# A vision tower with two routed expert layers: a first batch of 9 tiles, and its fixed units among the last tiles' routing

## The chip, the cores and the metric

The kernel runs on one core of a Trainium2 chip. The core has the engines TensorE (PE, matrix products; its weight loads are PEld), VectorE (DVE), ScalarE (ACT), GpSimd (POOL) and the sync engine (SP), each with its own in-order instruction stream; they meet through semaphores. In this kernel SP issues all plain transfers, and POOL issues the indirect ones (row gathers and scatters by an index per partition). The metric is the device time of one execution in microseconds (us), lower is better. Differences under half a per cent are not told from none.

## The reference

Everything is float32. 64 images of 3 x 96 x 96 are cut into 36 patches of 16 x 16 each and projected to 192 features; a class token is put in front, which makes 64 x 37 = 2368 rows. One attention block follows (12 heads, scores with a neighbour term subtracted before softmax), and then the part that this change is about, a feed-forward of two routed layers:

```python
h = h + attention(layernorm(h))
z = layernorm(h)
logits_fk = (z @ W_fk + b_fk) @ normalised(emb_fk).T        # 128 experts
logits_rk = (z @ W_rk + b_rk) @ normalised(emb_rk).T        # 128 experts
w_fk = top4_of(softmax(logits_fk)), scaled to sum 1         # the same for w_rk
hmid = sum over 4 experts n of w_fk[n] * (z @ f_know[n])    # f_know: 128 x 192 x 128
out  = h + sum over 4 experts n of w_rk[n] * (hmid @ r_know[n])   # r_know: 128 x 128 x 192
```

Both choices depend on z alone, so both are known before the first expert product.

## The kernel before, in words

**Attention.** Images go in 8 groups of 8 (`attention(g)` on PE, ACT and DVE, `group(g, more)` on POOL); each overlaps the embedding and projections of the next two. A finished group is stored to `h2_dram` and loaded back as tiles of 128 rows (`h2r`): 19 tiles, with the tiles that group g completes in `tiles_of(g + 1)`: 0-1, 2-3, 4-5, 6-8, 9-10, 11-12, 13-15, 16-18. In group g's instructions POOL first makes the neighbour sums of the next group (`sums`, lines 654 and 656; the second pair waits for `queries(g + 1)` on DVE) and the residual (line 664).

**Routing** of a tile: ACT normalises it (`route_x2`), PE transposes it (`route_transpose`), ACT copies (`route_T`), PE makes both routers' logits (`route_logits`), ACT copies (`route_logit`), DVE takes the top 8 and their indices and makes one-hot rows `hot` (`route_top`), ACT the exponentials (`route_exp`), and PE adds one-hots in bank 3: `ranks_before` gives each row its rank within its expert (copied by ACT, `route_rank`), `ranks_after` completes the count.

**Batches, plan, slots.** Tiles form two batches (`BATCHES`), here 0-10 and 11-18. When all of a batch are ranked, `plan(b, 0..3)` turns counts into a layout, DVE and PE alternating. Each expert has 32 rows of its own in a fixed part (4096 slots), and an expert with more rows gets whole blocks of 128 behind it. `slot(b, t, part)` on DVE (lines 1833 to 1846) turns ranks into slot numbers of a tile, four per router: part 0 has two operations over both routers' 256 columns and four picks, part 1 four picks and the end. POOL then scatters the tile's rows into `wide_dram[b]` by the first router's four slots (`scatter_x2`, line 697). In group 7 `slot_part()` puts parts of batch 0 between the steps of attention; what is left follows behind it. Plan 0 stands in group 6.

**Expert phases.** Four phases run in order: layer 0 with batch 0 and 1, layer 1 with batch 0 and 1 (`experts(ph)`). A step is four units of 256 slots; phases have 4 fixed steps and as many block steps as the plan says, in a loop over at most `STEPS`, with an `If`. A unit: SP loads the rows (`load_rows`, line 478), PE transposes (line 1114, banks 0 and 1), ACT copies (line 1398), PE multiplies (line 1129 fixed, 1140 block; banks 2 to 5), ACT copies (line 1389), SP stores the result in place (line 494). `expert_rows(ph, ahead)` on SP stores a phase's last units only behind the loads of the next phase, and these behind `ahead()`: for phase 0 the landing of all of batch 1's scatters, for phase 2 that of batch 1's mid rows. `expert_end(ph)` then releases POOL (line 547). PE starts phase 0 with 12 warm-up products (line 1147), and only once the second plan is done and all of `f_know` is loaded. `f_know` comes in 8 chunks of 1.5 MB: four during the last groups, four behind attention (its buffers lie under them). `r_know` comes in 8 chunks too: 5 in the second half of phase 1, between its last steps (first half of the experts done), 3 behind phase 1, ahead of `expert_end(1)`.

**Between layers** POOL gathers, for each tile, 4 results per row (`gather(0, b, t)`, line 710), DVE combines them (`combine`, line 1894), and POOL scatters the combination to `mid_dram` by the second router's four slots (`scatter_mid`, line 718). Gathers of a batch start when `experts_done[b]` is set. At the end `gather(1, b, t)` and `combine` give the output, which SP stores.

## Time and profile before

| | us |
|---|---|
| median of 3 runs | 803.53 |
| lowest, highest | 802.82, 807.34 |
| the profiled execution | 798.96 |
| its span, first to last instruction | 797.2 |
| PE busy | 547.9 (69%) |
| DVE busy | 384.0 (48%) |
| ACT busy | 339.5 (43%) |
| POOL busy | 403.4 (51%) |

One execution was profiled. The page has busy times, the span in 40 slices, DMA queues, the chain of work that ended last, the costliest groups and the DMA issues. A timeline lists instructions of an engine with start and duration; "[9.19 <-DVE diag L1805]" means that the engine stood idle for 9.19 us before it and what ended that. "issue" is a wait for nothing that the profile shows. L with a number is a line of the kernel. A row's last "x" is how many alike instructions were merged.

### The profile page before, as it was taken

To read this page: it belongs to the slowest core of one execution; us is meant where nothing else is said; L and a number is where in the kernel's file an instruction comes from. 1 tells how busy PE (TensorE), PEld (TensorE's weight loads), DVE (VectorE), ACT (ScalarE), POOL (GpSimd) and SP (SyncE) were. 2 spreads that over 40 slices of the span, in tenths; PEclk is the share of its full clock that TensorE was granted. 3 is DMA by queue.
4 is the path that set the end of the run, shared out by engine and by line. 5 is a ranking of instruction groups with operands and counts; after the bars stand their busy time and mean duration, and the time that the engine had idled before them with its cause. 6 is when DMAs were issued, how large, how long until landed. Compare 5 with 4: busy or idle time off the path is not lost.

```text
span 797.2 us, 16396 instructions
## 1 busy us (share of the span) xinstructions
PE 547.9 (69%) x5060; PEld 448.0 (56%) x5061; DVE 384.0 (48%) x1355; ACT 339.5 (43%) x738; POOL 403.4 (51%) x397
## 2 busy tenths in 40 slices
PE   6898999989898948704598868967119773776200
PEld 5686877869687826503377866757116462545200
DVE  1847678888697887999790001110101111023332
ACT  4246384764757545313355543533004552354100
POOL 3351450615232240576377006777767777366774
PEclk9789999999998977656599997995659998899655
DMA  5888679595870572397288756969998994699632
GB/s 141 305 333 348 211 302 348 198 414 198 343 299 14 120 154 49 90 259 210 74 239 265 208 158 177 260 193 323 318 297 244 281 278 137 204 279 267 197 94 72
DMA packets 151443, 177.44 MB, mean 223 GB/s; under 512 B 12778, under 2 KB 134931, under 8 KB 151379
## 3 DMA queue, kind: packets, MB, share of 16 engines
q1 hardware_dynamic: 138002, 149.20, 58.9%
q0 software_dynamic: 13376, 27.41, 11.9%
q8 instruction: 36, 0.59, 0.3%
q14 instruction: 29, 0.23, 0.1%
HBM read 76.55 MB, written 100.02 MB: 221 GB/s over the span
## 4 chain that ended last, share of the span: by engine, by line
PE 26%; POOL 22%; DVE 21%; issue 14%; ACT 10%; DMA 6%; SPq 1%; POOLq 0%; ACTq 0%; DVEq 0%
POOL gat L710 14%; POOL mid_dram L718 8%; PE bank L852 7%; DMA gat<-wide_dram,slots 5%; ACT qk_pad L1230 4%; PE bank L899 4%; DVE pick L1839 3%; PE bank L1140 3%; PE bank L1114 2%; PE bank L1129 2%; PE bank L837 2%; DVE smax L1616 2%; DVE probs L1619 1%; DVE acc L1894 1%; PE bank L960 1%
## 5 line engine op out<-in xcount | busy, mean ns | idle before, releaser
L710 POOL DMA_INDIRECT gat<-wide_dram,slots x152 | 145.3, 956 | 105.7 <-SPq L547 52.6
L1389 ACT ACTIVATE os<-bank 128x256 f32<-128x256 f32 (+1 forms) x160 | 70.1, 438 | 144.8 <-PE bank L1140 63.6
L1114 PE MATMUL bank<-ident,xs 128*96 128x128 f32 (+1 forms) x480 | 90.8, 303 | 46.3 <-issue 16.6
L654 POOL TENSOR_TENSOR qk_sum<-qk_pad 64x888 f32<-64x888 f32 x16 | 26.6, 1664 | 170.4 <-ACT qk_pad L1230 156.7
L1886 DVE TENSOR_SCALAR acc<-gat,wts 128x128 f32<-128x128 f32 x19 | 5.6, 297 | 222.3 <-DMA gat<-wide_dram,slots 222.3
L697 POOL DMA_INDIRECT wide_dram<-x2b,slots x76 | 77.1, 1015 | 61.9 <-issue 57.5
L1398 ACT ACTIVATE xsT<-bank 96x512 f32<-96x512 f32 (+1 forms) x160 | 76.1, 487 | 72.1 <-PE bank L1114 64.0
L1140 PE MATMUL bank<-matrices,xsT 96*128 (+1 forms) x576 | 102.8, 320 | 2.5 <-ACT xsT L1398 2.3
L1114 PEld LDWEIGHTS bank<-ident,xs 128*96 128x96 f32 (+1 forms) x480 | 60.5, 165 | 73.0 <-issue 42.0
L1140 PEld LDWEIGHTS bank<-matrices,xsT 96*128 96x128 f32 (+1 forms) x576 | 85.3, 209 | 9.0 <-issue 6.6
L718 POOL DMA_INDIRECT mid_dram<-comb,slots x76 | 74.2, 977 | 26.0 <-issue 22.9
L852 PE MATMUL bank<-tok_wT,pixT 128*128 128x192 f32 x384 | 69.5, 342 | 1.3 <-ACT pixT L1207 1.3
L1129 PE MATMUL bank<-matrices,xsT 96*32 96x128 f32 (+1 forms) x1536 | 63.5, 300 | 8.3 <-ACT xsT L1398 8.3
L852 PEld LDWEIGHTS bank<-tok_wT,pixT 128*128 128x128 f32 x384 | 67.5, 202 | 2.4 <-ACT pixT L1207 1.6
L1129 PEld LDWEIGHTS bank<-matrices,xsT 96*32 96x32 f32 (+1 forms) x1536 | 40.5, 112 | 22.0 <-ACT xsT L1398 12.1
L1147 PE MATMUL bank<-ones,ident 128*128 128x128 f32 x104 | 19.2, 370 | 47.7 <-DMA matrices<-in_L_ffn_r_know 33.1
L1894 DVE SCALAR_TENSOR_TENSOR acc<-gat,wts,h2r 128x192 f32<-128x192 f32 x19 | 8.0, 422 | 89.0 <-DMA gat<-wide_dram,slots 89.0
L1249 ACT ACTIVATE probs<-probs 101x444 f32<-101x444 f32 x32 | 18.3, 573 | 71.0 <-DVE probs L1619 70.9
L899 PE MATMUL bank<-w_vT,xnT_rep 96*111 96x192 f32 x256 | 44.7, 335 | 2.1 <-ACT xnT_rep L1218 2.1
L1147 PEld LDWEIGHTS bank<-ones,ident 128*128 128x128 f32 x104 | 18.6, 282 | 48.5 <-issue 48.5
L899 PEld LDWEIGHTS bank<-w_vT,xnT_rep 96*111 96x111 f32 x256 | 43.2, 181 | 2.4 <-ACT xnT_rep L1218 2.3
L1839 DVE SCALAR_TENSOR_TENSOR pick<-iota_n,idxf,srank 128x128 f32<-128x128 f32 x152 | 43.6, 349 | 0.7
(187 smaller groups left out, 980.7 us busy)
## 6 DMA issues: line engine op xcount, KB each, us to landing
wide_dram<-zeros SPq DMA_DIRECT2D x6, 5632.0 KB, 19.5
mid_dram<-zeros SPq DMA_DIRECT2D x8, 2816.0 KB, 25.7
xs<-wide_dram SPq DMA_DIRECT2D x80, 192.0 KB, 4.8
wide_dram<-os SPq DMA_DIRECT2D x80, 192.0 KB
matrices<-in_L_ffn_f_know SPq DMA_DIRECT2D x8, 1536.0 KB, 16.0
matrices<-in_L_ffn_r_know SPq DMA_DIRECT2D x8, 1536.0 KB, 14.7
wide_dram<-os SPq DMA_DIRECT2D x80, 128.0 KB
xs<-mid_dram SPq DMA_DIRECT2D x80, 128.0 KB
```

The lines of the kernel that those rows point to most:

```text
L697: pool.indirect_dma_start(wide_dram[b], bass.IndirectOffsetOnAxis(ap=slots[:, t, e:e + 1], axis=0), x2b[:, t - BATCHES[b][0], :], None)\
L710: pool.indirect_dma_start(gat[i][:, e, :], None, wide_dram[b], bass.IndirectOffsetOnAxis(ap=slots[:, t, k:k + 1], axis=0))\
L718: pool.indirect_dma_start(mid_dram[b], bass.IndirectOffsetOnAxis(ap=slots[:, t, TOPK + e:TOPK + e + 1], axis=0), comb[t % 2][:], None).the ...
L852: last = pe.matmul(bank[2 + 3 * f][:, t * D:(t + 1) * D], pixT[:, half, c, 2 * j:2 * j + 2, :].rearrange("p a n -> p (a n)"), tok_wT[:, kt ...
L899: last = pe.matmul(bank[VALUE_BANK[f]][0:VG * TOK, t * D:(t + 1) * D], xnT_rep[:, j * G_IMG + m].rearrange("p r n -> p (r n)"), w_vT[:, j, ...
L1114: last = pe.transpose(bank[r % 2][0:kp, c:c + ROWS], src, ident[:])
L1129: last = pe.matmul(bank[2 + r][q * FIRST:(q + 1) * FIRST, k * width:(k + 1) * width], xsT[r % 2][0:kp, c:c + FIRST], matrices[0:kp, at:at ...
L1140: last = pe.matmul(bank[2 + r][:, k * width:(k + 1) * width], xsT[r % 2][0:kp, c:c + ROWS], matrices[0:kp, bass.ds(starts[r * SB + k] + j ...
L1147: pe.matmul(bank[7][:, 0:ROWS], ident[:], ones[:], start=True, stop=True)
L1389: act.activation(os_[r][:, :, 0:width], bank[2 + r][:, 0:SB * width].rearrange("p (k w) -> p k w", w=width), ACT.Copy)\
L1398: act.activation(dst, src, ACT.Copy).then_inc(t_copied[ph], 1)
L1839: last = dve.scalar_tensor_tensor(pick[:, e, :], iota_n[:], idxf[:, t].rearrange("p r k -> p (r k)")[:, e:e + 1], srank[:, part * EXPERTS: ...
```

## The change

It does six things:

1. Batch 0 has tiles 0 to 8, batch 1 tiles 9 to 18; `ALL_STEPS` falls from 22 to 21.
2. Plan 0 needs group 5's ranks only. Its part 0 goes behind `queries(6)` on DVE in group 5, and parts 1 to 3 between group 6's softmax and finish steps; PE's parts go between the turns. The ranks of tiles 9 and 10, which start a new count in bank 3, move to the end of group 6.
3. `slot(b, t, r)` handles one router: 128 columns and four picks, end included. The first router's slots of batch 0 are made in group 6 (tiles 0 to 4) and group 7 (5 to 8); those of batch 1 behind plan 1; then all second-router slots (batch 0, batch 1), counted in `mid_slot_ready`. POOL waits for all 19 of these before it gathers for the mid rows. Ranks are int16.
4. PE and ACT start phase 0 as soon as attention has ended, batch 0's rows are loaded and `f_know`'s first four chunks are there: `first_phase()` puts the 16 fixed units among the routing of tiles 16 to 18, the ranks of 13 to 18 and plan 1. Banks: turned rows in 6 and 7, results in turn in 2, 4 and 5; routing keeps 0, 1 and 3. Phase 0 has no warm-up products.
5. SP loads the fifth `f_know` chunk, then the first rows, and the last three chunks between the row loads of steps 1 and 2 (`late_f`), each with a semaphore; PE waits for a chunk where a unit needs it. Scatters of batch 0 are counted in pairs of tiles.
6. `expert_end(1)` comes ahead of the last three `r_know` chunks.

```diff
-BATCHES = ((0, READY[5]), (READY[5], TTILES))
+BATCHES = ((0, READY[4]), (READY[4], TTILES))
...
-WARM = (12, 0, 24, 16)
+WARM = (0, 0, 24, 16)
+TURN_BANK = (6, 7)
+BESIDE_BANK = (2, 4, 5)
+BLOCK_BANK = ((0, 4, 5, 2), (2, 3, 4, 5), (2, 3, 4, 5), (2, 3, 4, 5))
...
-SLOTTED = {7: list(range(BATCHES[0][1]))}
+PLANNED = READY.index(BATCHES[0][1]) + 2
+SLOTTED = {6: list(range(5)), 7: list(range(5, BATCHES[0][1]))}
...
+            late = list(range(F_EARLY, EXPERTS // CHUNK))
+            def late_f():
+                if late:
+                    load_f([late.pop(0)])
+            late_f()
 
...
-                def next_rows(s, first=False):
+                def next_rows(s, first=False, beside=None):
...
+                        if beside and r % 2 == 1:
+                            beside()
 
                 for s in range(1, FIXED):
-                    next_rows(s, s == 1)
+                    next_rows(s, s == 1, late_f if ph == 0 else None)
...
-            for t in range(*BATCHES[0]):
-                sp.wait_ge(scattered[t], 64)
-            sp.wait_ge(plan_ev[1], 4)
+            for n in range(PAIRS):
+                sp.wait_ge(scattered[n], PAIR_ROWS[n])
             for r in range(RING):
                 load_rows(0, 0, r)
             expert_rows(0, rows_of_second)
             expert_end(0)
             expert_rows(1, None)
+            expert_end(1)
             for n in range(EXPERTS // CHUNK - EARLY):
                 load_r(EARLY + n, r_late[n])
-            expert_end(1)
             mid_rows(0)
             for r in range(RING):
                 load_rows(2, 0, r)
...
+                pool.wait_ge(mid_slot_ready, TTILES)
...
+                planned = g == PLANNED
                 scores(g, 0)
                 scores(g, 1)
-                if n_old > 0:
+                if planned:
+                    plan(0, 0)
+                elif n_old > 0:
                     ranks_before(old[0])
...
+            def units(lo, hi):
+                for u in range(lo, hi):
+                    s, r = divmod(u, RING)
+                    turned_rows(0, *divmod(u + 1, RING))
+                    if u == 0:
+                        pe.wait_ge(f_early, 16 * F_EARLY)
+                    elif u % 2 == 0 and u >= 2 * F_EARLY:
+                        pe.wait_ge(f_late[u // 2 - F_EARLY], 16)
+                    first_products(0, s, r, bank[BESIDE_BANK[(u + 2) % 3]], 3)
+            def first_phase():
+                last_tiles, end_tiles = tiles_of(GROUPS - 1), tiles_of(GROUPS)
+                pe.wait_ge(consts, 4)
+                pe.wait_ge(o_read, TILES * GROUPS + 1)
+                pe.wait_ge(scores_read, TILES * GROUPS + 2)
+                pe.wait_ge(plan_ev[0], 4)
+                used = steps_of(0)
+                for t in last_tiles:
+                    ranks_before(t)
+                    ranks_after(t)
+                turned_rows(0, 0, 0)
+                units(0, 4)
+                for t in end_tiles:
+                    route_transpose(t)
+                units(4, 6)
+                for t in end_tiles:
+                    route_logits(t)
+                units(6, 10)
+                for n, t in enumerate(end_tiles):
+                    ranks_before(t)
+                    units(10 + n, 11 + n)
+                    ranks_after(t)
+                for part in range(3):
+                    units(13 + part, 14 + part)
+                    plan(1, part)
+                block_steps(0, used, FIXED, 3)
...
+            def second_rows(t):
+                lo = BATCHES[1][0]
                 if t - lo < BATCHES[0][1]:
-                    act.wait_ge(scattered[t - lo], 64)
+                    act.wait_ge(scattered[(t - lo) // 2], PAIR_ROWS[(t - lo) // 2])
                 act.activation(x2b[:, t - lo, :], h2r[:, t, :], ACT.Identity,
                                bias=nb2[:, t:t + 1], scale=rs2[:, t:t + 1]).then_inc(xb_ready, 1)
 
+            def units(lo, hi):
+                for u in range(lo, hi):
+                    if u + 1 < FIXED * RING:
+                        turned(0, *divmod(u + 1, RING))
+                    results(0, *divmod(u, RING), bank[BESIDE_BANK[(u + 2) % 3]])
+            def first_phase():
+                last_tiles, end_tiles = tiles_of(GROUPS - 1), tiles_of(GROUPS)
+                for t in last_tiles:
+                    route_exp(t)
+                    route_rank(t)
+                turned(0, 0, 0)
+                units(0, 2)
+                for t in end_tiles:
+                    route_x2(t)
+                units(2, 4)
+                for t in end_tiles:
+                    route_T(t)
+                units(4, 6)
+                for t in end_tiles:
+                    route_logit(t)
+                for u in range(6, 16):
+                    if 10 <= u < 13:
+                        route_exp(end_tiles[u - 10])
+                        route_rank(end_tiles[u - 10])
+                    units(u, u + 1)
+                    second_rows(BATCHES[1][0] + u - 6)
...
-                parts = [(t, h) for t in SLOTTED.get(g, []) for h in range(2)]
+                parts = [(t, 0) for t in SLOTTED.get(g, [])]
...
+                if g == PLANNED:
+                    plan(0, 1)
+                else:
+                    slot_part()
                 softmax_in(g, 2)
-                slot_part()
+                if g != PLANNED:
+                    slot_part()
                 softmax_in(g, 3)
                 if len(old) > 2:
                     route_top(old[2])
-                slot_part()
+                if g == PLANNED:
+                    plan(0, 2)
+                else:
+                    slot_part()
                 finish(g, 0)
-                slot_part()
+                if g == PLANNED:
+                    plan(0, 3)
+                else:
+                    slot_part()
                 finish(g, 1)
                 if old:
                     weights(old)
                 slot_part()
                 finish(g, 2)
-                if planned:
-                    plan(0, 0)
                 slot_part()
                 finish(g, 3)
                 slot_part(8)
                 if more > 0:
                     queries(g + 1)
                     slot_part()
-                    if planned:
-                        plan(0, 1)
-                        plan(0, 2)
+                    if g + 1 == PLANNED:
+                        plan(0, 0)
...
+            def slot(b, t, r):
+                n = 3 * (r * TTILES + t)
+                here = rank[b][:, t - BATCHES[b][0], r * EXPERTS:(r + 1) * EXPERTS]
+                dve.scalar_tensor_tensor(moved[:], here, float(FIRST), base_b[b][:, r * EXPERTS:(r + 1) * EXPERTS],
+                                         ALU.is_ge, ALU.mult).then_inc(slot_step, 1)
+                dve.wait_ge(slot_step, n + 1)
+                dve.tensor_tensor(srank[:], here, moved[:], ALU.add).then_inc(slot_step, 1)
+                dve.wait_ge(slot_step, n + 2)
+                for k in range(TOPK):
                     last = dve.scalar_tensor_tensor(
+                        pick[:, k, :], iota_n[:], idxf[:, t, r, k:k + 1], srank[:],
+                        ALU.is_equal, ALU.mult, accum_out=slotf[t % 2][:, k:k + 1])
+                last.then_inc(slot_step, 1)
+                dve.wait_ge(slot_step, n + 3)
+                dve.scalar_tensor_tensor(slots[:, t, r * TOPK:(r + 1) * TOPK], idxf[:, t, r, :], float(FIRST),
+                                         slotf[t % 2][:], ALU.mult, ALU.add)\
+                   .then_inc((slot_ready, mid_slot_ready)[r], 1)
...
-            for t in range(*BATCHES[1]):
-                for half in range(2):
-                    slot(1, t, half)
+            for r in range(2):
+                for b in range(1 - r, 2):
+                    for t in range(*BATCHES[b]):
+                        slot(b, t, r)
```

## Rows read from the trace of the kernel before

**Rows 1.** The page's part 4, the chain that ended last, by line.
```profile
POOL gat L710 14%; POOL mid_dram L718 8%; PE bank L852 7%; DMA gat<-wide_dram,slots 5%; ACT qk_pad L1230 4%; PE bank L899 4%; DVE pick L1839 3%; PE bank L1140 3%; PE bank L1114 2%; PE bank L1129 2%; PE bank L837 2%; DVE smax L1616 2%; DVE probs L1619 1%; DVE acc L1894 1%; PE bank L960 1%
```

**Rows 2.** Windows of two stretches: busy us of each engine, clock, DMA.
```profile
278.00:314.00 36.00, 21.74 (x165) 17.20 (x165) 28.60 (x69) 18.07 (x38) 8.98 (x5) 0.76 0.45 91
350.00:394.00 44.00, 17.23 (x74) 9.98 (x74) 37.97 (x187) 16.71 (x59) 26.50 (x25) 0.58 0.62 166
```

**Rows 3.** POOL's timeline (start us, us), its first and last DMAs of each stage.
```profile
324.56 1.60 POOL L697 DMA_INDIRECT wide_dram<-x2b,slots  x1 [25.49 <-issue]
...
385.53 0.96 POOL L697 DMA_INDIRECT wide_dram<-x2b,slots  x1 [0.30 <-issue]
397.29 0.95 POOL L697 DMA_INDIRECT wide_dram<-x2b,slots  x1 [10.79 <-issue]
...
437.17 0.96 POOL L697 DMA_INDIRECT wide_dram<-x2b,slots  x1 [0.30 <-issue]
481.11 0.98 POOL L710 DMA_INDIRECT gat<-wide_dram,slots  x1 [42.98 <-SPq L547]
...
595.78 0.98 POOL L710 DMA_INDIRECT gat<-wide_dram,slots  x1 [0.30 <-issue]
...
676.03 0.97 POOL L718 DMA_INDIRECT mid_dram<-comb,slots  x1 [0.30 <-issue]
...
749.06 0.95 POOL L710 DMA_INDIRECT gat<-wide_dram,slots  x1 [0.36 <-issue]
...
788.47 0.95 POOL L710 DMA_INDIRECT gat<-wide_dram,slots  x1 [0.30 <-issue]
```

**Rows 4.** DVE's timeline, the last operation of the second plan.
```profile
393.03 0.16 DVE L1827 TENSOR_SCALAR steps_used<-steps_f 1x2 int32<-1x2 f32 x1
```

**Rows 5.** DVE's timeline in group 6: a plan operation and the queries.
```profile
288.18 1.77 DVE L1797 CAST nblk<-nblk_i 128x2 bf16<-128x2 int32 x1
...
291.01 2.39 DVE L1646 TENSOR_SCALAR qk_pad<-bank,qk_scale,qk_bias 64x296 f32<-64x296 f32 x4
```

**Rows 6.** POOL's timeline in group 6: a sum and the residual.
```profile
287.99 1.93 POOL L656 TENSOR_TENSOR qk_pad<-qk_pad,qk_sum 64x888 f32<-64x888 f32 x1
...
297.27 1.80 POOL L664 TENSOR_TENSOR h_res<-h,v_bias 101x768 f32<-101x768 f32 x1
```

**Rows 7.** DVE's timeline: first operation of two whole slots in a row.
```profile
361.01 0.42 DVE L1833 SCALAR_TENSOR_TENSOR moved<-rank,base_b 128x256 f32<-128x256 f32 x1
...
364.31 0.42 DVE L1833 SCALAR_TENSOR_TENSOR moved<-rank,base_b 128x256 f32<-128x256 f32 x1
```

**Rows 8.** The DMA view's issues: engine, op, count, KB each, median us to landing.
```profile
xs<-wide_dram SPq DMA_DIRECT2D x80, 192.0 KB, 4.8
...
wide_dram<-x2b,slots POOLq DMA_INDIRECT x76, 3.4
```

**Rows 9.** PE's timeline: products of a fixed unit and of two block steps' firsts.
```profile
400.69 1.08 PE L1129 MATMUL bank<-matrices,xsT 96*32 96x128 f32 x32 [0.25 <-ACT xsT L1398]
...
428.94 1.15 PE L1140 MATMUL bank<-matrices,xsT 96*128 x8
...
435.59 1.15 PE L1140 MATMUL bank<-matrices,xsT 96*128 x8 [0.23 <-ACT xsT L1398]
```

**Rows 10.** ACT's timeline: first turned rows and first result of phase 1.
```profile
482.93 0.59 ACT L1398 ACTIVATE xsT<-bank 96x512 f32<-96x512 f32 x1 [6.93 <-PE bank L1114]
...
485.68 0.38 ACT L1389 ACTIVATE os<-bank 128x256 f32<-128x256 f32 x1 [1.30 <-PE bank L1129]
```

**Rows 11.** SP's timeline: phase 1's first row load, its chunks, its last stores.
```profile
472.62 0.37 SPq L478 DMA_DIRECT2D xs<-wide_dram  x1
...
549.27 16.57 SPq L483 DMA_DIRECT2D matrices<-in_L_ffn_r_know  x4
574.86 4.81 SPq L494 DMA_DIRECT2D wide_dram<-os  x5
```

**Rows 12.** PE's timeline in group 6: the plan's product.
```profile
299.41 1.22 PE L989 MATMUL bank<-diag,ones 128*128 128x128 f32 x4 [9.19 <-DVE diag L1805]
```

More of the change, by code:

```diff
@@ new lines, in turned_rows @@
+            def turned_rows(ph, s, r):
+                layer = PHASES[ph][0]
+                kp, parts = ((DH, 2), (RANK, 1))[layer]
+                pe.wait_ge(xs_loaded[ph][r], 16 * (s + 1))
+                pe.wait_ge(t_copied[ph], s * RING + r + 1)
+                for k in range(SB):
+                    for j in range(parts):
+                        src = xs[r][:, k, j:D:2] if layer == 0 else xs[r][:, k, 0:RANK]
+                        c = k * 256 + j * ROWS
+                        last = pe.transpose(bank[TURN_BANK[r % 2]][0:kp, c:c + ROWS], src, ident[:])
+                last.then_inc(t_filled[ph], 1)
@@ new lines, in block_steps @@
+            def block_steps(ph, used, first, depth):
+                with pe.Fori(first, ALL_STEPS) as s, pe.If(s < used):
+                    starts = block_starts(ph, s)
+                    for r in range(RING):
+                        if r + 1 < RING:
+                            turned_rows(ph, s, r + 1)
+                        else:
+                            with pe.If(s + 1 < used):
+                                turned_rows(ph, s + 1, 0)
+                        products(ph, s, r, starts, bank[BLOCK_BANK[ph][r]], depth)
```

307 lines of the change are left out of this document (127 added, 180 removed).

## The prediction

> **What bounds the kernel now.** First the page. Of the chain that ended last 14% is line 710 and 8% line 718, POOL's indirect gathers and scatters of the expert stage [rows 1]: the last 316 us are paced by one queue of 1 us DMAs. Next the windows by stage [rows 2]: from 350 to 394 PE is busy 17 of 44 us, DVE 38, so VectorE's slots and routing keep TensorE from the experts. Then POOL's timeline as a calendar [rows 3]: the 44 scatters of batch 0 start at 324.56 and end at 386.5, the 32 of batch 1 start at 397.29, the gathers of batch 0 at 481.11 (held by SP line 547, the end of phase 0), those of batch 1 at 595.78 without a wait, the last scatter of mid rows starts at 676.03, layer 1 gathers start at 686.60 and run to 788.47; the span ends 8.7 us later. I call the end of the second plan P; here it is 393.2 [rows 4], and the kernel ends at P + 404.
>
> Counting the reference's top-4 choices of these inputs by expert (pad rows too) gives the steps. Now: layer 0 has 53 and 40 blocks, 7 and 5 block steps; layer 1 has 51 and 38, 7 and 5; with 4 fixed steps each that is the x80 loads per layer of the page. With 9 + 10 tiles: layer 0 has 41 and 48 blocks, 6 and 6 steps; layer 1 has 39 and 47, 5 and 6 steps. A step is 4 units, a tile has 4 rows DMAs of each kind.
>
> **Part 1: up to the first unit of phase 0.** Its rows need all 36 scatters of batch 0. These follow, on POOL's queue, sums(7,1) and residual(7), which wait for `queries(7)` on DVE. Now `queries(7)` ends at 293.4, and POOL is through 5.7 us later, at 299.1 [rows 5, 6]. After, DVE has before it:
> - five half slots. One whole slot now takes 3.30 us (361.01 to 364.31): 0.45 + 0.46 for 256 columns, 8 picks at 0.273, 0.2 for the end [rows 7]. Half of it, at 128 columns: about 0.31 + 0.32 + 1.09 + 0.2 = 1.94, so 9.7. (Bounds 1.65, exactly half, and 2.2, with no gain from the narrower first two; int16 input, which no row shows, I take at nothing.)
> - plan parts 1 to 3, moved before `queries`: 1.1 + 1.0 + 1.0, of which about 1 falls into gaps where DVE waits for PE: +2.1.
> - plan part 0 leaves: from 285.48, where diag starts, to 289.9, so -4.4 [rows 5]. It goes into group 5: 1.5 net plus what POOL's sums cost there, +2 (bounds 0, as DVE waits for POOL just behind, to 4).
> - POOL's sums hold up small DVE operations: nblk, on 128x2 values, takes 1.77 us under POOL's 287.99 operation [rows 5, 6]. The slots now lie there: +3 (bounds 0 and 3.6, the two operations' length).
>
> The Trainium skill, "SBUF — State Buffer", section "Who interferes with whom", with "SBUF: two separate sides", says that the port pair shared by DVE and GpSimd is locked for a whole instruction, also against DVE operations with two SBUF inputs when the GpSimd operation reads SBUF; the picks are such. By it the last term is 3.6, and without it 0: it speaks against putting slots into group 6, since in group 7 POOL only issues DMAs.
>
> Sum +12.4: `queries(7)` ends at 305.8, POOL is free at 311.5, first scatter at 312. A scatter's pitch is 1.27 clean, (385.53 - 324.56 - 2.65) / 43 = 1.36 on the mean [rows 3]; I take 1.32: 35 x 1.32 + 1 = 47.2, to 359.2. Landing 3.4, issue 0.4, row load 4.8 [rows 8]: unit 0 starts at 368, bounds 359 and 373. That is 31 us before today's 399.4. PE, ACT and the hots of tiles 13 to 15 are ready by about 348, so they don't decide; that 11 slots (36 us) in group 7 and its tail become 4 half ones (7.8) thus gains nothing by itself.
>
> **Part 2: the interleaved units, and P.** A warm fixed unit is 1.63 us PE to PE (400.69 to 402.32) and 1.77 with the joints of four ((428.94 - 400.69) / 16) [rows 9]. PE has idled 20 us and has lost its 12 warm-up products (5.3 us); after such a pause the first two units of phase 1 took 2.8 each at the lower clock (482.93 to 485.68 [rows 10]). So units 0 to 3: 8.9. PE then runs in order: transposes of three tiles 1.3 + 1.2 for the two-bank ring; units 4, 5: 3.5; logits 6 x 0.43 = 2.6 + 0.5; units 6 to 9: 7.1; units 10 to 12, each with ranks before and after. There ACT is slower than PE: exp 1.35 + rank 0.38 + turned 0.59 + result 0.39 + x2b 0.45 = 3.2 each, 9.6; units 13 to 15 with plan products 5.3 + 1.1; last plan part on DVE 1.6. Sum 42.7, I take 43: P = 411. (The small operations' durations are those of the timelines of 361 to 393.) The f_know chunks 5 to 7 are 4.7 MB in the first 12 us of this, beside 320 KB per unit; four such chunks held SP 15.5 us from 339.7, and row loads queue behind them, but routing gives the slack. Bounds: 38 (routing at its bare PE time) and 50 (3 chunks at the 3.6 us that a unit waited in phase 1, less the overlap). P between 399 and 420.
>
> So starting 31 us earlier ends with P 18 us *later*: batch 0's fixed units now stand in front of the plan that the second batch needs.
>
> **Part 3: from P to the end.** Batch 1's scatters: DVE's first half slot and the wake-up 2.7, then 39 x 1.286 + 1 = 51.1 ((437.17 - 397.29) / 31 = 1.286), landing 3.4: P + 57.2. Today this ends at 441 and hides behind phase 0 (to 473); now phase 0 has 24 block units left, 6 x 6.65 = 40 (428.94 to 435.59 [rows 9]), ends at P + 38 and waits. SP stores its last rows only behind that wait, so gathers of batch 0 start 8.5 us later (472.6 to 481.1), at P + 65.7; DVE's 29 half slots end at P + 56 and are hidden by it. From SP's first load of the next phase to the first copy of turned rows took 10.3 us (472.6 to 482.93 [rows 10, 11]): phase 1 starts at P + 67.5.
>
> Phase 1 today: 482.93 to its last store's issue at 579.3 = 96.4, of which the last 30 go to r_know chunks on SP (16.57 us for four) and the loop behind them [rows 11]. With 10 steps in place of 9, chunk 2 can't follow chunk 1 at once at 549: a step's row loads come between, and they follow PE's units of the step before, which end at 561. SP would be through with the chunks at 577 rather than 565.8: +11. 107.4, landing and wake-up 3.4: gathers of batch 1 at P + 178.3. That line 547 now comes ahead of the late chunks takes 9 us of SP's time off this; today it is hidden, as POOL comes to 595.78 without waiting. POOL itself would be through batch 0 at P + 65.7 + 72 x 1.27 + 4 = P + 161: phase 1 takes over as the bound, POOL idles 17 us.
>
> Batch 1 on POOL: (676.03 - 595.78) / 63 = 1.274; 79 x 1.274 = 100.6: last mid scatter at P + 278.9. Phase 2 (36 units, late chunks from P + 178, start about P + 201) is done near P + 255, hidden. Tail from there today 121.2; plus 4 units of phase 3, 6.6, plus 8 gathers at (788.47 - 749.06) / 31 = 1.271, 10.2: 138.0. End: P + 416.9, against P + 404.
>
> **Sum.** 411 + 416.9 = 828 span, against 797.2: +31. The profiled execution took 798.96; the median of the three runs is 803.53, 4.6 above it, so 803.5 + 31 = 834.
>
> **Rivals.**
> 1. *POOL stays the bound of batch 0*: chunks on SP don't hold phase 1 longer than POOL needs. For: line 710 and 718 run without a gap through 561 to 595. Against: phase 1 begins level with batch 0's gathers, as today, but has one step more and POOL 16 DMAs less. It takes 17 off: 817.
> 2. *Faster*: the front wins. Place: the attention of group 6, which sheds the 9.2 us in which PE waits for plan's diag and ACT 14 us for logits [rows 12]. If DVE's slots fit into these gaps, scatters start at 299, as POOL is free then, unit 0 at 355, and with routing at its bare 38 us P is 393; with rival 1 that gives 393 + 400 = 793, time 799. It decides at P below 397 with rival 1, below 380 without. Against: DVE itself is busy 28.6 of 36 us in 278 to 314 [rows 2] and takes 9.7 more.
> 3. *Later still*: f chunks starve the interleaved units (P 420) and r chunks clog batch 1's gathers at their start (two waits of 6 to 7 us for a gather stand in the chain at 561 and 581): 845, time 850.
> 4. *No change*: P near 396 with rival 1.
>
> **Chances.** Forecast 0.48, rival 1 0.19, rival 3 0.13, rival 2 0.14, rival 4 0.06. Half a per cent (4 us) is what a measurement can tell here. Faster 0.14, same 0.06, slower 0.80. The range 806 to 848 leaves out rival 2, rival 4 and the worst of 3.
>
> **What would show it.** Scatters of batch 0 begin near 312 and end near 359; unit 0's first transposes near 368 at half clock; P near 411; POOL idle between batch 0's last and batch 1's first scatter; PE idle about 25 us between phases 0 and 1; POOL waiting 10 to 20 us for SP's `experts_done` before batch 1's gathers; the last mid scatter near 690; 40 gathers at the end. P at or under 395, or no wait before batch 1's gathers, would make the forecast wrong.

## The result and the profile after

The changed kernel takes 824.38 us (median of 4 runs, 822.99 to 830.05) against 803.17 (800.36 to 807.34) beside it: ratio 1.027, 95% interval 1.022 to 1.032. It is slower, by 21 us; 834 was forecast, with a range of 806 to 848. The profiled execution spans 822.0 us (before 797.2), 828 was forecast. The ratios here and below leave disturbed executions out; the profiled ones of e3 and e9 are such, so their spans are longer than their ratios say.

POOL's timeline of the changed kernel, read as the calendar of [rows 3] (start us, us, line, operation, idle time before it and what ended it):

```profile
292.88 1.66 POOL L661 TENSOR_TENSOR qk_sum<-qk_pad 64x888 f32<-64x888 f32 x1 [26.16 <-ACT qk_pad L1278]
294.63 1.92 POOL L663 TENSOR_TENSOR qk_pad<-qk_pad,qk_sum 64x888 f32<-64x888 f32 x1
309.46 1.66 POOL L661 TENSOR_TENSOR qk_sum<-qk_pad 64x888 f32<-64x888 f32 x1 [12.92 <-DVE qk_pad L1722]
...
362.02 0.96 POOL L704 DMA_INDIRECT wide_dram<-x2b,slots  x1 [0.30 <-issue]
422.49 0.96 POOL L704 DMA_INDIRECT wide_dram<-x2b,slots  x1 [59.52 <-DVE slots L1924]
...
472.85 1.04 POOL L704 DMA_INDIRECT wide_dram<-x2b,slots  x1 [0.30 <-issue]
484.21 0.98 POOL L717 DMA_INDIRECT gat<-wide_dram,slots  x1 [10.32 <-SPq L555]
...
581.79 0.97 POOL L717 DMA_INDIRECT gat<-wide_dram,slots  x1 [5.14 <-SPq L555]
...
684.03 0.97 POOL L725 DMA_INDIRECT mid_dram<-comb,slots  x1 [0.30 <-issue]
695.86 0.97 POOL L717 DMA_INDIRECT gat<-wide_dram,slots  x1 [10.86 <-SPq L555]
...
763.52 0.94 POOL L717 DMA_INDIRECT gat<-wide_dram,slots  x1 [18.17 <-SPq L555]
```

VectorE's timeline has the factors of the end tiles and, 65 us later, the end of the second plan, P = 419.8 (before 393.2 [rows 4]):

```profile
354.25 0.15 DVE L1670 SCALAR_TENSOR_TENSOR nb<-mv,rr 128x3 f32<-128x3 f32 x1
...
419.60 0.16 DVE L1907 TENSOR_SCALAR steps_used<-steps_f 1x2 int32<-1x2 f32 x1
```

Call g0 and g1 the first layer-0 gathers of batch 0 and batch 1, M the last scatter of mid rows. The difference of the spans splits at these marks:

| stretch | before | after | forecast |
|---|---|---|---|
| start to P | 393.2 | 419.8 | 411 |
| P to g0 | 87.9 | 64.4 | 65.7 |
| g0 to g1 | 114.7 | 97.6 | 112.6 |
| g1 to M | 80.3 | 102.2 | 100.6 |
| M to the end | 121.2 | 138.0 | 138.0 |

Two terms were off, P by +8.8 and g0 to g1 by -15.0. The rest is within 2 us. Over P, TensorE's timeline of the interleaved units (transposes of the rows, the first of each unit) has the reason:

```profile
367.02 1.95 PE L1108 MATMUL bank<-ident,xs 128*96 128x128 f32 x8 [12.21 <-DMA xs<-wide_dram]
...
377.31 0.60 PE L1108 MATMUL bank<-ident,xs 128*96 128x128 f32 x4
383.07 1.10 PE L1108 MATMUL bank<-ident,xs 128*96 128x128 f32 x4 [4.15 <-DMA xs<-wide_dram]
...
400.97 1.10 PE L1108 MATMUL bank<-ident,xs 128*96 128x128 f32 x4 [4.46 <-DMA xs<-wide_dram]
```

and SP's timeline over the same time shows what held the rows:

```profile
364.42 4.95 SPq L484 DMA_DIRECT2D xs<-wide_dram  x6
...
371.75 0.47 SPq L447 DMA_DIRECT2D matrices<-in_L_ffn_f_know  x1
372.26 0.87 SPq L484 DMA_DIRECT2D xs<-wide_dram  x1
...
375.75 0.92 SPq L447 DMA_DIRECT2D matrices<-in_L_ffn_f_know  x1
376.71 6.51 SPq L484 DMA_DIRECT2D xs<-wide_dram  x1
...
386.31 1.11 SPq L447 DMA_DIRECT2D matrices<-in_L_ffn_f_know  x1
387.47 5.29 SPq L484 DMA_DIRECT2D xs<-wide_dram  x1
```

A chunk itself is issued in about a microsecond. Behind the first of the three a row load takes 0.87 us. Behind the second and third it takes 6.51 and 5.29, and the units run dry. The DMA engines' share was 0.63 from 371 to 375 and 1.10 from 375 to 376.5: the long issues fall into the time in which the engines are full. The windows around the first wait (length, busy us of PE, PEld, DVE, ACT, POOL, granted clock, DMA share, GB/s) show the second price:

```profile
376.00:379.00 3.00, 2.58 (x50) 1.85 (x42) 0.00 (x0) 2.07 (x6) 0.00 (x0) 1.00 1.10 240
379.00:383.00 4.00, 0.00 (x0) 0.00 (x0) 0.00 (x0) 0.37 (x1) 0.00 (x0) 0.85 1.12 287
383.00:388.00 5.00, 4.93 (x41) 3.72 (x42) 0.00 (x0) 0.98 (x2) 0.00 (x0) 0.50 1.10 228
```

TensorE stands still for 4 us, and in the next 5 it is granted half its clock, the 1.2 GHz level: four transposes take 1.10 us where they took 0.60.

### The profile page after: what moved, and what is told of

Same layout as the page of the kernel before. It is cut to its first block, busy times and chain, and to the rows that moved or that the text cites. A ratio compares the mean times of both kernels' runs of the same rounds, so it can differ in the third digit from the quotient of the medians.

```text
span 822.0 us, 16234 instructions
## 1 busy us (share of the span) xinstructions
PE 547.7 (67%) x5012; PEld 446.4 (54%) x5013; DVE 391.0 (48%) x1412; ACT 337.0 (41%) x732; POOL 402.4 (49%) x397
## 3 DMA queue, kind: packets, MB, share of 16 engines
q0 software_dynamic: 13376, 27.41, 11.3%
## 4 chain that ended last, share of the span: by engine, by line
PE 25%; POOL 19%; DVE 15%; issue 15%; DMA 12%; ACT 9%; SPq 3%; ACTq 1%; POOLq 0%; DVEq 0%
POOL wide_dram L704 8%; POOL gat L717 8%; PE bank L860 7%; DMA xs<-wide_dram 5%; PE bank L1122 4%; ACT qk_pad L1278 4%; POOL mid_dram L725 4%; PE bank L1108 3%; DMA xs<-mid_dram 3%; PE bank L907 3%; PE bank L1144 2%; PE bank L845 2%; DMA gat<-wide_dram,slots 2%; DVE smax L1692 2%; DMA wide_dram<-os 2%
## 5 line engine op out<-in xcount | busy, mean ns | idle before, releaser
L1422 ACT ACTIVATE os<-bank 128x256 f32<-128x256 f32 (+1 forms) x156 | 67.9, 435 | 172.0 <-DMA wide_dram<-os 72.9
L661 POOL TENSOR_TENSOR qk_sum<-qk_pad 64x888 f32<-64x888 f32 x16 | 26.6, 1663 | 187.5 <-ACT qk_pad L1278 164.5
L1144 PE MATMUL bank<-matrices,xsT 96*128 (+1 forms) x560 | 96.7, 313 | 1.7 <-ACT xsT L1416 1.6
L1144 PEld LDWEIGHTS bank<-matrices,xsT 96*128 96x128 f32 (+1 forms) x560 | 80.4, 204 | 7.2 <-issue 4.9
L1122 PE MATMUL bank<-matrices,xsT 96*32 96x128 f32 (+1 forms) x1536 | 67.9, 315 | 10.3 <-ACT xsT L1416 10.3
L860 PE MATMUL bank<-tok_wT,pixT 128*128 128x192 f32 x384 | 71.9, 350 | 1.3 <-ACT pixT L1255 1.3
L860 PEld LDWEIGHTS bank<-tok_wT,pixT 128*128 128x128 f32 x384 | 70.1, 209 | 2.5 <-ACT pixT L1255 1.6
L1122 PEld LDWEIGHTS bank<-matrices,xsT 96*32 96x32 f32 (+1 forms) x1536 | 42.8, 117 | 26.1 <-ACT xsT L1416 13.5
L1208 PE MATMUL bank<-ones,ident 128*128 128x128 f32 x80 | 14.7, 371 | 57.2 <-DMA mid_dram<-comb,slots 30.3
L1919 DVE SCALAR_TENSOR_TENSOR pick<-iota_n,idxf,srank 128x128 f32<-128x128 f32 x152 | 47.7, 370 | 1.3
L1208 PEld LDWEIGHTS bank<-ones,ident 128*128 128x128 f32 x80 | 14.3, 283 | 57.7 <-issue 57.7
```

What stands on the lines that cost most here:

```text
L860: last = pe.matmul(bank[2 + 3 * f][:, t * D:(t + 1) * D], pixT[:, half, c, 2 * j:2 * j + 2, :].rearrange("p a n -> p (a n)"), tok_wT[:, kt ...
L1122: last = pe.matmul(out_bank[q * FIRST:(q + 1) * FIRST, k * width:(k + 1) * width], xsT[r % 2][0:kp, c:c + FIRST], matrices[0:kp, at:at + w ...
L1144: last = pe.matmul(out_bank[:, k * width:(k + 1) * width], xsT[r % 2][0:kp, c:c + ROWS], matrices[0:kp, bass.ds(starts[r * SB + k] + j * R ...
L1422: act.activation(os_[r][:, :, 0:width], out_bank[:, 0:SB * width].rearrange("p (k w) -> p k w", w=width), ACT.Copy)\
L1919: last = dve.scalar_tensor_tensor(pick[:, k, :], iota_n[:], idxf[:, t, r, k:k + 1], srank[:], ALU.is_equal, ALU.mult, accum_out=slotf[t % ...
```

## The experiments

Theories. A: the change is slower because the order puts units in front of the plan (P), and because 9 and 10 tiles make batch 1 the long chain. Rivals: the split alone; the chunk loads; phase 0's own length. Twelve more kernels were run. The table has them with the marks of their traces (P the end of the second plan, g0, g1 and M as above):

| kernel | ratio to before | P | g0 | g1 | M | span |
|---|---|---|---|---|---|---|
| changed kernel | 1.027 [1.022, 1.032] | 419.8 | 484.2 | 581.8 | 684.0 | 822.0 |
| e1 split alone | 1.023 [1.016, 1.029] | 388.2 | 468.8 | 572.9 | 675.2 | 811.7 |
| e2 route first | 1.013 [1.007, 1.019] | 379.6 | 471.2 | 578.1 | 680.0 | 817.8 |
| e3 route mix | 1.002 [0.999, 1.006] | 381.9 | 467.3 | 570.3 | 672.5 | 812.1 |
| e4 chunks first | 1.025 [1.019, 1.030] | 414.6 | 479.0 | 580.2 | 682.3 | 824.5 |
| e5 end behind | 1.043 [1.037, 1.050] | 422.2 | 486.0 | 593.6 | 697.1 | 835.3 |
| e6 f on ACT | 0.985 [0.977, 0.992] | 386.9 | 453.4 | 552.9 | 655.1 | 795.4 |
| e7 gap scatter | 0.990 [0.984, 0.995] | 385.9 | 456.7 | 557.1 | 659.1 | 793.6 |
| e8 eleven | 1.015 [1.010, 1.020] | 387.6 | 492.9 | 606.7 | 686.7 | 806.3 |
| e9 eleven, chunks first | 0.982 [0.976, 0.988] | 390.0 | 476.9 | 588.9 | 672.0 | 795.7 |
| e10 gap, mix, chunks first | 0.992 [0.987, 0.996] | 390.7 | 457.3 | 557.7 | 659.7 | 800.5 |
| e11 later r | 0.979 [0.975, 0.984] | 388.9 | 456.2 | 547.7 | 649.9 | 786.7 |
| e12 f on ACT, later r | 0.979 [0.975, 0.984] | 387.3 | 453.8 | 545.3 | 647.3 | 783.2 |

The first scatters of kernels with the same front begin between 314.7 and 320.1: marks of two traces compare to some 5 us, ratios to about 1%.

**e1, the split alone** (kernel before):

```diff
-BATCHES = ((0, READY[5]), (READY[5], TTILES))
+BATCHES = ((0, READY[4]), (READY[4], TTILES))
```

> The kernel before with one edit: batches of 9 and 10 tiles in place of 11 and 8. Theory A (the split by itself is a loss of about 18 us, and the rest of the change has to earn it back): batch 0's scatters end near 376; P, the end of the second plan, comes 4 to 7 us earlier (two whole slots less on DVE ahead of it), 386 to 389; gathers of batch 0 at P + 81; gathers of batch 1 now wait for SP and start near P + 186 (before: P + 203); last mid scatter P + 287; then a tail of about 138 in place of 121: span about 813, ratio 1.015 to 1.025. Theory B (the split costs nothing, the loss of the change is all in the interleaved order): span 790 to 797, ratio 0.99 to 1.00.

POOL's timeline:

```profile
468.79 0.98 POOL L710 DMA_INDIRECT gat<-wide_dram,slots  x1 [24.65 <-SPq L547]
...
572.88 0.98 POOL L710 DMA_INDIRECT gat<-wide_dram,slots  x1 [11.43 <-SPq L547]
...
753.14 0.94 POOL L710 DMA_INDIRECT gat<-wide_dram,slots  x1 [18.25 <-SPq L547]
```

Theory A: P 388.2, g0 at P + 80.6, g1 at P + 184.7, span 811.7 against 813. That the span comes so near is partly chance: the profiled execution, with 813.4, was the fastest of four (up to 827.1). Two waits for SP are new beside [rows 3]: POOL used to go on at g1 and at the last batch's layer-1 gathers without a wait (595.78 and 749.06). Batch 0 now has 36 DMAs of each kind where it had 44, so POOL is there early, and with one more step phases 1 and 3 are done late. So on the old order the split costs 2.3%, nearly the whole loss of the change.

**e2 and e3, the order alone** (changed kernel). TensorE's part of e2 follows, ScalarE's has the same order. In e3 `turned_rows(0, 0, 0)` stands ahead of the plan, units 0 to 2 ahead of its three products, units 3 to 15 behind. ScalarE's staging of batch 1's rows (`second_rows`) starts behind unit 6 in e2, as in the changed kernel, and behind unit 0 in e3.

```diff
-                turned_rows(0, 0, 0)
-                units(0, 4)
                 for t in end_tiles:
                     route_transpose(t)
-                units(4, 6)
                 for t in end_tiles:
                     route_logits(t)
-                units(6, 10)
-                for n, t in enumerate(end_tiles):
+                for t in end_tiles:
                     ranks_before(t)
-                    units(10 + n, 11 + n)
                     ranks_after(t)
                 for part in range(3):
-                    units(13 + part, 14 + part)
                     plan(1, part)
+                turned_rows(0, 0, 0)
+                units(0, 16)
```

> The changed kernel with one edit on PE and ACT: the routing of tiles 16 to 18 and the products of plan 1 stand ahead of all 16 fixed units of phase 0, instead of between them. Theory A (the units that stand in front of the plan are what makes it late): x2 of the end tiles at 354.5, when DVE has their factors, tops 359 to 367, P at 378 to 382 (changed kernel: 419.8); batch 1's first scatter near 382, its last near 433; POOL idles 19 us there, not 60; phase 0's fixed units run from 377 to 416, its block steps to 456, gathers of batch 0 near 464 (changed kernel: 484.2); the rest keeps its length: span about 802, ratio about 1.005. Theory B (phase 0's own length or the split decides, the place of the plan does not): P moves, but gathers of batch 0 stay at 480 to 486 and the span at 820 to 824, ratio 1.025.

> The changed kernel with the routing of tiles 16 to 18 ahead of the units, and only units 0 to 2 between the three products of plan 1, units 3 to 15 behind. Theory A: P at 380 to 385, unit 0 at 368 as in the changed kernel, fixed units done by 408 to 412, block steps by 452, gathers of batch 0 near 458 to 461: span about 797, ratio 0.99 to 1.00, some 4 us below the kernel with all units behind. Theory B (the place of the plan does not decide): span 820 to 824.

P fell by 38 to 40 us in both, as expected. In the changed kernel x2 of the end tiles stood behind two units on ScalarE, though its factors were ready at 354.4. ScalarE's timelines, the changed kernel's first:

```profile
373.14 1.41 ACT L1312 ACTIVATE x2t<-h2r,nb,rs 128x192 f32<-128x192 f32 x3
```

then e2's:

```profile
356.86 1.42 ACT L1308 ACTIVATE x2t<-h2r,nb,rs 128x192 f32<-128x192 f32 x3 [0.75 <-DVE nb L1664]
```

In e2 POOL's first scatter of batch 1 waited until 21 us behind P for the staged rows; in e3 it went out at 384.6. POOL in e2:

```profile
400.70 0.96 POOL L704 DMA_INDIRECT wide_dram<-x2b,slots  x1 [35.32 <-ACT x2b L1434]
```

That wait did not set g0. In both kernels SP starts phase 1's row loads 6.2 us behind the last store of its loop (e2: 455.90 to 462.09; e3: 452.38 to 458.57, when batch 1's scatters had ended 22 us before). In the changed kernel, where the scatters' landing does hold SP, it is 25.5 us (449.84 to 475.36). So with P out of the way phase 0 itself ends last, and e2 ends it 3.5 us later than e3. Why e2's ratio is 0.011 above e3's is shown only as far as its marks go: g0 is 3.9 us later, g1 7.8.

The order, with the staging that goes with it, is worth 2.4% (1.027 to 1.002). It is less than P's 38 us, since phase 0 ends last in e3 (POOL waits 31.3 us for SP before g0) and it had three waits for rows, 11.3 us.

**e4, chunks first** (changed kernel): all late f_know chunks ahead of the first rows.

```diff
-            late_f()
+            while late:
+                late_f()
```

> The changed kernel with the four late f_know chunks all issued before the first row loads (as before the change) instead of one there and three among the row loads of phase 0. Theory A (the chunks ahead of row loads on SP's queue cost the two waits of 4.15 and 4.46 us and the low clock behind them): both waits go, unit 0 stays near 367, P falls from 419.8 to 408 to 412, and everything behind it with it: span 812, ratio 1.012 to 1.016. Theory B (the chunks' traffic costs the same wherever it lies): batch 0's scatters or the first rows come 4 to 9 us later, P within 3 us of 419.8, ratio 1.025.

Both theories hold in part: no unit waits and P is 5 us earlier, but the rows of unit 0 come 9.5 us later, and the ratio doesn't move. From unit 0 to P it is 38.0 us, in the changed kernel 52.8: that is the price of the two stops, 14.8 us. The 5 us that P gains are lost again, 3.6 between g0 and g1 and 4.2 behind M; why is not shown. TensorE's timeline, and DMA in e4's window (share next to last):

```profile
376.57 1.74 PE L1109 MATMUL bank<-ident,xs 128*96 128x128 f32 x7 [23.78 <-DMA xs<-wide_dram]
```

```profile
346.00:364.00 18.00, 4.81 (x20) 2.49 (x20) 7.15 (x37) 3.87 (x18) 11.76 (x13) 0.50 1.08 302
```

The DMA engines are full (share 1.08) while the chunks run beside the scatters.

**e5, the release back behind the r_know chunks** (changed kernel):

```diff
             expert_rows(1, None)
-            expert_end(1)
             for n in range(EXPERTS // CHUNK - EARLY):
                 load_r(EARLY + n, r_late[n])
+            expert_end(1)
```

> The changed kernel with expert_end(1) back behind the three late r_know chunks on SP. Theory A (the prediction's 9 us): SP's release of batch 1's gathers comes behind three chunk issues of 7.6 us, gathers of batch 1 start at 590 (changed kernel: 581.8, after a wait of 5.1), and as batch 1 is the longest chain the whole end moves with them: span 830, ratio 1.035. Theory B (phase 1 is paced elsewhere; the kernel with the split alone had this old order and its gathers of batch 1 came 104 us behind those of batch 0, no later than in two kernels with the new order, 103 and 107): within 3 us of 824, ratio 1.024 to 1.030.

SP's timeline and POOL's g1:

```profile
581.35 2.97 SPq L500 DMA_DIRECT2D wide_dram<-os  x5
584.37 7.27 SPq L489 DMA_DIRECT2D matrices<-in_L_ffn_r_know  x3
```

```profile
593.56 0.97 POOL L717 DMA_INDIRECT gat<-wide_dram,slots  x1 [14.01 <-SPq L555]
```

Theory A: g0 to g1 is 107.6 against 97.6, and the end goes with it. The ratio, 1.043, is above the 1.035 expected, as g0 was 1.8 us later too. This part of the change is worth 1.6%, a gain inside a loss. Before the change it was hidden, as POOL came to g1 without a wait.

**e6, chunks from another queue** (e3, the ScalarE part behind the ranks of tile 15):

```diff
-            late = list(range(F_EARLY, EXPERTS // CHUNK))
+            late = [F_EARLY]
...
                     route_rank(t)
+                act.wait_ge(res_used, GROUPS + 1)
+                act.wait_ge(stored, 64 * GROUPS + 1)
+                for n in range(F_EARLY + 1, EXPERTS // CHUNK):
...
+                    act.dma_start(dst, f_view[:, n * CHUNK:(n + 1) * CHUNK, :]).then_inc(f_late[n - F_EARLY], 16)
```

> The kernel e3_route_mix with f_know chunks 5 to 7 issued by ScalarE behind the ranks of tile 15 (near 354), not by SP among the row loads. Theory A (it is SP's queue: a row load issued behind a chunk takes 5 to 6.5 us to issue): the waits of the units (4.5 + 3.6 + 3.3 us in e3) go, unit 0 starts with the rows as before, fixed units end 11 us sooner, gathers of batch 0 near 457, span 801, ratio 0.990. Theory B (it is the traffic: with all chunks ahead of the rows unit 0 came 9.5 us later): unit 0 comes 6 to 10 us later, no waits behind it, gathers of batch 0 within 3 us of 467, ratio 1.00.

The waits went and g0 came at 453.4, a little better than theory A's numbers. The mechanism is not the queue alone. ScalarE was held as SP had been, and unit 0 came 4 us later (8, counted from the first scatter), as theory B had it:

```profile
353.34 7.84 ACTq L1455 DMA_DIRECT2D matrices<-in_L_ffn_f_know  x3
```

The DMA engines were no less busy for it, with a share of 1.03 to 1.10 from 353 to 377. What pays is one late start in place of three stops, each with its stretch at half clock: ScalarE's first to 16th copy of turned rows took 25.3 us, in e3 43.5 and in e2 42.8.

**e7, scatters in POOL's gap** (e3, with units 0 to 5 between ranks and plan products; `between` holds tiles 0 and 1):

```diff
                     sums(g + 1, 0)
+                    if between:
+                        pool.wait_ge(cat_ready, 2 * (g + 1) + 1)
+                    for t in between:
+                        scatter_x2(0, t)
+                    if between:
+                        pool.wait_ge(scattered[0], 128)
                     sums(g + 1, 1)
```

> The kernel e3_route_mix with two edits for an earlier phase 0: POOL scatters tiles 0 and 1 in its idle 12.9 us between sums(7,0) and sums(7,1) (it waits for these scatters to land before sums(7,1)), and units 0 to 5 stand between the ranks and plan products of the end tiles. Counted on e3's trace: scatters of batch 0 end 8 us sooner, unit 0 at 364 to 366 (e3: 373.5), P near 384, phase 0 done 7 to 9 us sooner, gathers of batch 0 near 460, end 804: ratio 0.990 to 0.995. If phase 0's end does not decide (rival: batch 1's own chain from P does), P and the end stay: ratio 1.00 to 1.005.

```profile
300.70 1.19 POOL L710 DMA_INDIRECT wide_dram<-x2b,slots  x1 [1.70 <-issue]
...
312.27 1.66 POOL L661 TENSOR_TENSOR qk_sum<-qk_pad 64x888 f32<-64x888 f32 x1 [1.44 <-DMA wide_dram<-x2b,slots]
```

As expected: in POOL's timeline eight scatters fill the stretch before sums(7,1), which they hold up by 1.4 us; unit 0 starts at 364.0, g0 is at 456.7. e7 has two edits, the scatters and the place of the units, and does not tell them apart.

**e8 and e9, 11 and 8 tiles with the rest of the change** (routing first, all of batch 1's rows staged ahead of the units, plan 0 where it was; e9 with all late f_know chunks first):

```diff
-BATCHES = ((0, READY[4]), (READY[4], TTILES))
+BATCHES = ((0, READY[5]), (READY[5], TTILES))
...
-SLOTTED = {6: list(range(5)), 7: list(range(5, BATCHES[0][1]))}
+SLOTTED = {7: list(range(BATCHES[0][1]))}
...
```

> The changed kernel's half slots, 16-bit ranks and routing-first order, but batches of 11 and 8 tiles, plan 0 where it was before the change, all slots of batch 0 in group 7. Against the kernel before it says what the rest of the change is worth without the split. Theory A (the split is the loss, and half slots take 15 us off VectorE ahead of P): P near 379, batch 1's scatters follow batch 0's at once (386 to 427), unit 0 near 397 as before, gathers of batch 0 at 473 to 479, those of batch 1 at 586 to 591, no wait before the last gathers, span 789 to 793, ratio 0.990 to 0.995. Theory B (with the plan early, 9 and 10 tiles are as good as 11 and 8): ratio 1.00 to 1.005, as e3.

> The kernel e8_eleven with the four late f_know chunks all issued before the first row loads, as the kernel before has them. Theory A (e8's loss was the chunks among the row loads: its phase 0 took 86.5 us from first to last copy of turned rows, before 71.5, with three waits of 4.6 to 5.3 us): waits go, phase 0 takes 70 to 73, gathers of batch 0 at 476 to 480, span 789 to 793, ratio 0.990 to 0.996. Theory B (the loss lies elsewhere, as in phase 1): ratio 1.012 to 1.017 again.

e8 was a miss: POOL waits for phase 0 longer than before. TensorE's timeline in e8 shows why, the pattern of the changed kernel again:

```profile
398.14 0.68 PE L1111 MATMUL bank<-ident,xs 128*96 128x128 f32 x4
404.79 1.10 PE L1111 MATMUL bank<-ident,xs 128*96 128x128 f32 x4 [4.96 <-DMA xs<-wide_dram]
407.69 1.10 PE L1111 MATMUL bank<-ident,xs 128*96 128x128 f32 x4
```

A chunk costs (407.69 - 398.14) - 2 x 1.63 = 6.3 us of phase 0 [rows 9]. e9 takes the chunks away from there. Its fixed units take 18 us less and the ratio is 3.3% lower, at 0.982 better than the 0.990 to 0.996 of theory A. The rows of unit 0 are due only at 391, and from 356 to 391 the DMA share was 0.20 to 0.32 in e8: there is idle DMA time for the chunks, which e4 and e10 don't have. So the rest of the change, with the chunks first, gains 1.8% without the split.

The split's 2.3% belongs to the old order. With routing first, 9 and 10 tiles (e2, 1.013) and 11 and 8 (e8, 1.015) are level within their intervals, though e8 stages its rows earlier, and e9 (0.982) is level with e6 (0.985).

**e10 and e11** (e3's order, e7's scatters, chunks first; e11 with r_know chunks 2 to 4 behind the release of batch 1's gathers):

```diff
-                        load_r(n, r_early)
+                        if n < 2:
+                            load_r(n, r_early)
...
             expert_end(1)
+            for n in range(2, EARLY):
+                load_r(n, r_early)
```

> 9 and 10 tiles, the order of e3_route_mix (routing first, units 0 to 2 between the plan's products), tiles 0 and 1 scattered in POOL's idle stretch before sums(7,1), and all f_know chunks issued by SP before the first row loads. Theory A (the three gains add): scatters of batch 0 end near 354, unit 0 at 370 to 373, P at 379 to 383, no wait for rows, phase 0 66 us long, gathers of batch 0 at 447 to 449, span 787 to 790, ratio 0.978 to 0.983. Theory B (they share one resource, the DMA engines, which are full while the chunks run, so that earlier scatters only land later): unit 0 at 377, gathers of batch 0 near 453 and ratio 0.985 to 0.990, as in e6_f_on_act.

> The kernel e10_gap_mix_chunks with r_know chunks 2 to 4 issued behind expert_end(1), with the late ones, instead of ahead of phase 1's last stores. Theory A (three chunk issues, 9 to 11 us on SP at the end of phase 1, hold the release of batch 1's gathers): POOL's wait before batch 1's gathers (6 to 7 us) goes, they start 92 to 94 us behind those of batch 0 (all kernels so far: 97 to 107), span 6 us under e10's, ratio 0.007 lower. Theory B (phase 1 itself is late, not its stores): no change against e10; or phase 2, whose matrices come later, pushes phase 3 and the last gathers wait longer than 21 us.

e10 was the other miss, on the side of theory B and beyond it (0.992 where B had 0.985 to 0.990): batch 0's scatters end at 353.5, and still its rows are not there before 380.4. SP's timeline and the window:

```profile
346.80 15.19 SPq L447 DMA_DIRECT2D matrices<-in_L_ffn_f_know  x4
362.22 20.54 SPq L485 DMA_DIRECT2D xs<-wide_dram  x6
```

```profile
346.00:364.00 18.00, 12.40 (x50) 7.05 (x48) 13.71 (x62) 10.26 (x39) 6.62 (x7) 0.64 1.00 257
364.00:380.00 16.00, 4.46 (x20) 1.92 (x20) 6.18 (x25) 3.16 (x15) 0.00 (x0) 0.56 1.07 220
```

Six row loads take 20.5 us to issue behind four chunks. e11 is theory A: POOL doesn't wait at g1, 91.5 us behind g0, which is the 72 DMAs of batch 0 at 1.27 each. The ratio falls by 0.013 where 0.007 was expected; 8.9 us of it lie between g0 and g1, and 4 us behind M, which the theory did not have. SP's timeline in e10 and in e11:

```profile
535.31 8.59 SPq L490 DMA_DIRECT2D matrices<-in_L_ffn_r_know  x3
...
552.25 3.03 SPq L501 DMA_DIRECT2D wide_dram<-os  x5
```

```profile
531.84 10.71 SPq L501 DMA_DIRECT2D wide_dram<-os  x6
544.23 22.87 SPq L490 DMA_DIRECT2D matrices<-in_L_ffn_r_know  x6
```

**e12, the best of both** (e6 with e11's edit):

> The kernel e6_f_on_act (routing first, f_know chunks 5 to 7 issued by ScalarE, ratio 0.985) with r_know chunks 2 to 4 issued behind expert_end(1), the edit by which e11_later_r stands 0.013 under e10. Theory A (SP's chunk issues ahead of phase 1's last stores cost 7 to 10 us on top of everything else): gathers of batch 1 start 93 us behind those of batch 0 with no wait for SP, span 786 to 788, ratio 0.972 to 0.976, the fastest kernel of the study. Theory B (e11's gain was chance or belongs to its own timing): within 0.004 of 0.985.

```profile
545.31 0.98 POOL L720 DMA_INDIRECT gat<-wide_dram,slots  x1 [0.30 <-issue]
...
724.70 0.94 POOL L720 DMA_INDIRECT gat<-wide_dram,slots  x1 [16.72 <-SPq L556]
```

787.6 us, with e11 the fastest of the study: 2.1% under the kernel before. Against e6 the ratio falls by 0.006, about half of what was expected, and the intervals overlap. POOL's wait before the last gathers, 16 to 23 us, stands in every kernel with 9 and 10 tiles, and nothing was tried on it. Nor was 11 and 8 tiles (e9) tried with e11's edit, so which split is the better one in the end stays open.

## Why the prediction was right or wrong

**The sign and its main reason: right.** "Starting 31 us earlier ends with P 18 us later: batch 0's fixed units now stand in front of the plan." P came 26.6 us later, unit 0 at 367.0 (forecast 368), and e2 and e3, which change that order only, take P back to 380 and 382.

**Part 1: right, its error small.** `queries(7)` ended at 309.3, not 305.8. A half slot takes 1.95 us (forecast 1.94); the first, beside POOL's sums at 292.88, takes 5.15, which is the +3 of the sum: two of its picks took 1.76 and 2.06 us, where a pick beside no sum took 0.35. On VectorE's timeline the half slot lies between these rows:

```profile
292.02 0.28 DVE L1913 SCALAR_TENSOR_TENSOR moved<-rank,base_b 128x128 f32<-128x128 int16 x1
...
297.01 0.16 DVE L1924 SCALAR_TENSOR_TENSOR slots<-idxf,slotf 128x4 int32<-128x4 f32 x1
298.02 0.28 DVE L1913 SCALAR_TENSOR_TENSOR moved<-rank,base_b 128x128 f32<-128x128 int16 x1
```

The prediction weighed this term at 3.6 us by the Trainium skill's rule on the shared port ("SBUF — State Buffer", section "Who interferes with whom") and at 0 without it. The trace agrees with the rule: 3.2 us more beside 3.58 us of POOL's two sums. The scatters of batch 0 began 4 us late, at 316.25, and ended 4 us late, at 363.0. The cause of `queries(7)`'s 3.5 us stays open; they are less than the 5.4 us by which the first scatters of kernels with the same front differ. That unit 0 came at 367.0 even so is luck: from the end of the last scatter to the first transpose it took 4.0 us, where 3.4 + 0.4 + 4.8 = 8.6 was counted.

**Part 2: P was mis-sized by 8.8.** "Row loads queue behind them, but routing gives the slack" is the sentence that failed. The routing gave none, as TensorE's queue holds routing and units in one order: a unit that waits holds the logits behind it. There were two stops of 4.15 and 4.46 us, and behind each two units at half clock; e8 has such a chunk at 6.3 us. From unit 0 to P it took 52.8 us where 43 was forecast, and in e4, without the stops, 38.0: the routing and the units cost 5 less than was counted, the stops, which the sum had at nothing, 14.8. The trace of the kernel before had such stops, of 5.29 us at 536.02 and 3.63 at 550.37 (TensorE, line 1114); the prediction used only the smaller, and only for a bound. Its bound of 420 held P, and so did rival 3's first half, "f chunks starve the interleaved units (P 420)".

**Part 3: g0 right, g0 to g1 15 us too long.** "+11" for the r_know chunks failed. The forecast took the 16.57 us of four chunks in a row [rows 11] and a step more between. In the trace of the changed kernel a step stands between them, and the issues cost less (why is not shown):

```profile
557.86 9.79 SPq L489 DMA_DIRECT2D matrices<-in_L_ffn_r_know  x3
...
576.00 3.38 SPq L500 DMA_DIRECT2D wide_dram<-os  x5
```

Chunk 2 cost 0.69 at 548.91, and SP was through at 567.7, not 577. Phase 1 took 95.4 us from its first copy to its last store where 107.4 was forecast: 12 of the 15 us. The other 3 are its start, level with g0 and not 1.8 us behind it, and its release, 2.4 us behind the last store and not 3.4. "Takes 9 us of SP's time off this" was right (e5: 10), "today it is hidden" too. So POOL waited 5 us, not 17: nearer to rival 1, in which POOL doesn't wait at all, than to the forecast.

**The tail: right to the tenth** (138.0), and that is partly luck, as its account of it wasn't whole: it is an 18.2 us wait for phase 3 in front of 40 gathers, in place of more gathers in front of them.

**The split:** the prediction told of it under part 3 only. e1 shows that it alone makes 2.3% in the old order, and e9 that the rest, with the units behind the plan and chunks ahead, gains. The faster rival's own path was not taken: it had the scatters start at 299 and unit 0 at 355, and they came at 316.25 and 367.0. What beats the kernel before is another order: e3 and e6 reach P at 382 to 387, and e6, with the chunks out of the row loads, has a ratio of 0.985.

The two errors, +8.8 and -15, have nothing to do with each other; that they cancel in part, and leave the span 5.9 us under the forecast, is luck. Of the 9.6 us between 834 and 824.4, 5.9 are the span's. The rest is the 4.6 us added for the median, which turned out 0.6 above the profiled execution.

## What to carry to other kernels

When work is pulled forward into an in-order queue, ask what it now stands in front of: here 16 units came in front of the plan on which the longer chain hung, and the order was worth 2.4%. A wait that costs nothing today has a price once its cover goes (e5), so price each one with and without it. Large loads belong where the DMA engines are idle (e9), or at least not between short loads that the engines wait for (e6), and behind the release that others wait for (e11).

## What the runs showed of the hardware

- In the changed kernel the three late 1.5 MB loads took 0.47, 0.92 and 1.11 us to issue, and the 192 KB load behind each 0.87, 6.51 and 5.29 us. The DMA share was 0.63 around the first and 1.10 to 1.11 around the others. On ScalarE's queue three such loads held ScalarE for 7.84 us.
- With the DMA share at 1.07, six loads of 192 KB took 20.5 us to issue (e10), against 4.95 for six in the changed kernel, where it was 0.53.
- In 4 us without work TensorE's granted clock was 0.85 on the mean, and in the next 5 us, at work again, 0.50.
- Beside GpSimd's sums of 1.66 and 1.92 us, two VectorE picks took 1.76 and 2.06 us, against 0.35 without.
- Four chunks in a row held SP for 16.57 us [rows 11]; with a step between the first and the rest, 0.69 + 9.79.
